# Image 3's routing rounds hold tiles 0, 1 and 2 to 4 in place of 0 to 2 and 3, 4, in a fused embed, attention and expert kernel whose five work orders are laid out anew

## The reference

```python
h = jnp.einsum('bhid,oi,od->bho', x, weighted_sum, weight)
h = jnp.concatenate([h, txt], axis=1)
# attention, on layernorm(h)
gk = jax.nn.log_sigmoid(x @ Wg1 @ Wg2 + bg2).reshape(Bb, Ll, H, D) / GLN
def step(S, inp):
    S = jnp.exp(gk_t)[..., None] * S + k_t[..., None] * v_t[..., None, :]
    o_t = jnp.einsum('bhdv,bhd->bhv', S, q_t) * SCALE
o = o * jax.lax.rsqrt(jnp.mean(o * o, axis=-1, keepdims=True) + EPS) * g_norm_w
o = o.reshape(Bb, Ll, Hid)
h = h + (o * (g * jax.nn.sigmoid(g))) @ Wo
# experts, on layernorm(h)
top_v, top_i = jax.lax.top_k(xf @ Wr, K)                 # K = 2
expv = jnp.exp(top_v - m)
top_p = expv / (jnp.sum(expv, axis=-1, keepdims=True) + 1e-12)
oh = experts[:, None] == jnp.arange(E)[None, :]
pos = jnp.sum(jnp.cumsum(oh.astype(jnp.int32), axis=0) * oh, axis=-1) - 1
kept = pos < cap
xe = jnp.zeros((E, cap + 1, D)).at[experts, pos_safe].set(xf[tokens])[:, :cap]
h2 = jax.nn.silu(xe @ W1) * (xe @ W3)                     # per expert
ye = h2 @ W2
out = jnp.zeros((T, D)).at[tokens].add(wk[:, None] * yp)  # h + out is returned
```

## Time and profile before

| | us |
|---|---|
| median of 3 runs | 599.27 |
| lowest, highest | 598.28, 599.59 |
| the profiled execution, its own time | 594.9 |
| its span, first to last instruction | 593.1 |
| of that: up to the end of attention and routing | 266 |
| `early_up` and the wait behind it | 266 to 282 |
| the eight experts | 282 to 593 |

### The profile page before, as it was taken

One profiled execution on the slowest core, in us unless ns is written; L12 is line 12 of the kernel. 1 busy time (PEld: TensorE's weight loads), 2 busy tenths in 40 slices (PEclk: granted clock), 3 DMA queues, 4 the chain that ended last, 5 costly groups with the idle time before them and its releaser, 6 DMA issues.

```text
span 593.1 us, 13905 instructions
## 1 busy us (share of the span) xinstructions
PE 568.7 (96%) x4846; PEld 531.2 (90%) x4846; DVE 385.0 (65%) x1007; ACT 335.0 (56%) x891; POOL 337.0 (57%) x394
## 2 busy tenths in 40 slices
...
GB/s 266 236 277 123 149 11 51 72 54 23 81 73 64 70 23 65 70 89 110 164 161 90 187 119 7 263 33 71 214 17 186 116 5 264 34 66 77 19 2 48
DMA packets 44587, 60.09 MB, mean 101 GB/s; under 512 B 4529, under 2 KB 33137, under 8 KB 44530
## 3 DMA queue, kind: packets, MB, share of 16 engines
...
...
## 4 chain that ended last, share of the span: by engine, by line
PE 82%; DVE 8%; ACT 3%; issue 3%; DMA 2%; SPq 0%; POOL 0%; DVEq 0%; POOLq 0%; ACTq 0%
PE ps L1950 45%; PE ps L1997 15%; PE ps L2191 3%; PE ps L2177 3%; PE ps L1992 3%; PE ps L2136 2%; PE ps L2172 2%; PE ps L1971 1%; PE ps L2184 1%; DMA sb_x_in<-in_x 1%; PE ps L2152 1%; PE ps L2206 1%; DVE sb_bn L1555 1%; DMA sb_h<-in_txt 1%; PE ps L2225 1%
## 5 line engine op out<-in xcount | busy, mean ns | idle before, releaser
L1950 PE MATMUL ps<-sb_xe_hi,sb_rounded 128*128 128x256 f32 (+1 forms) x1024 | 206.2, 296 | 0.0
L1950 PEld LDWEIGHTS ps<-sb_xe_hi,sb_rounded 128*128 128x128 f32 x1024 | 166.0, 190 | 0.0
L1950 PE MATMUL ps<-sb_xe_lo,sb_rounded 128*128 128x320 f32 (+1 forms) x512 | 151.6, 296 | 0.0
L1950 PEld LDWEIGHTS ps<-sb_xe_lo,sb_rounded 128*128 128x128 f32 x512 | 97.2, 190 | 0.0
L1997 PE MATMUL ps<-sb_rounded,sb_h_hi 128*128 128x256 f32 x512 | 94.2, 285 | 0.0
L1460 DVE TENSOR_TENSOR sb_dec<-ps,sb_gate 128x256 f32<-128x256 f32 (+1 forms) x121 | 55.2, 456 | 54.3 <-ACT sb_gate L1164 51.0
L1164 ACT ACTIVATE sb_gate<-ps 128x256 f32<-128x256 f32 (+1 forms) x121 | 49.2, 406 | 66.3 <-PE ps L1950 65.4
L1997 PEld LDWEIGHTS ps<-sb_rounded,sb_h_hi 128*128 128x128 f32 x512 | 78.4, 189 | 0.0
L998 POOL DMA_INDIRECT out_rows<-sb_att,sb_s_token x40 | 61.8, 1545 | 29.0 <-DVE sb_att L1471 22.6
L1490 DVE TENSOR_TENSOR sb_h_lo<-sb_dec,sb_h_hi 128x256 fp32r<-128x256 f32 x128 | 69.8, 546 | 3.7 <-ACT sb_h_hi L1425 3.2
L1997 PE MATMUL ps<-sb_rounded,sb_h_lo 128*128 128x256 f32 x256 | 72.0, 281 | 0.0
...
## 6 DMA issues: line engine op xcount, KB each, us to landing
...
```

Source lines behind the costliest of these rows:

```text
L1950: ins = pe.matmul(out_ap, lhs, rhs, start=(first and i == 0), stop=(last and i == n - 1))
```

## The change

`ROUNDS` moves tile 2 of image 3 (number 17) from round 4 to round 5, and all five tables of orders are new. The work is the same: the same steps, except that the two rounds have other lengths. Several steps are done by another engine: `ln2_apply` of six tiles goes to ACT from POOL or DVE; of the splits and gated outputs at the start and through the images some go from DVE or ACT to POOL and others back.

```diff
-ROUNDS = [(0, 5), (5, 10), (10, 13), (13, 15), (15, 18), (18, 20)]
+ROUNDS = [(0, 5), (5, 10), (10, 13), (13, 15), (15, 17), (17, 20)]
...
-xn2_turn.3.2@7 attn_out.3.3@6 rank.3@4 router.3.2@5 attn_out.3.4@7 rank.4@6 xn2_turn.3.3@5 xn2_turn.3.4@4 router.3.3@7
-router.3.4@5 early_turn.1@4 early_turn.0@6 early_turn.2@7 rank.5@5 early_up.1@2 early_up.0@0 counts@4 early_up.3@6
...
+xn2_turn.3.2@1 attn_out.3.4@4 router.3.2@6 attn_out.3.3@5 rank.4@7 xn2_turn.3.3@4 xn2_turn.3.4@6 router.3.3@5
+router.3.4@4 rank.5@6 counts@7 early_turn.0@5 early_turn.1@4 early_turn.2@2 early_up.0@0 early_up.1@6 early_up.2@2
...
-x_split.0.2.0 x_split.0.2.1 wo_scale x_split.0.3.0 x_split.1.0.1 x_split.1.1.0 x_split.1.3.1 q_mask.0.0 x_split.2.0.1
...
+we_split.2 we_split.3 x_split.0.2.1 x_split.0.2.0 x_split.0.3.1 x_split.0.3.0 wo_scale x_split.1.0.0 x_split.1.1.1
```

More of the change, by code:

```diff
@@ L55 @@
[L55 to L69, removed]
```

229 lines of the change are left out of this document (122 added, 107 removed).

## The result

The changed kernel takes 600.61 us (median of 19 runs, 596.34 to 603.99) against 597.62 us (19 runs, 593.28 to 600.47) for the kernel before: ratio 1.0056, 95% interval 1.0033 to 1.0079. That is +3.3 us, slower. The forecast was slower by 1.8 us, 601.1 in a range of 596.4 to 604.2; sign and range held, the size was about half of what came. That 601.1 lies so near to 600.61 is luck: the forecast started from 599.27, the median of three runs of the kernel before, and over 19 runs that median is 597.62.

The account below looks back on a forecast made before the run. PE's own work was taken as the bound, except at attention's end, where a chain over DVE, PE and ACT sets the time. Terms 0.5 + 0 + 1.0 - 0.6 + 0.85 = +1.75 gave 601.1 us, range 596.4 to 604.2.

Parts of the forecast that it names:

- (f): End of attention: early_turn goes behind rank.5, slots.5 and counts, so early_up waits on DVE; +3.3 us.
- (a): End of attention: ACT copies turned tiles sooner, PE's last steps close up behind a short wait before mix.3.3; -0.65 us.
- (b): End of attention: limits.4 no longer needs the last tile and its top2 holds two, ending earlier; -1.2 us.
- (d): Round 5 gets three tiles: rank.5 +0.85 us and its top2 +0.4 us.
- (e): End of attention: limits.5 no longer stands behind weigh.5 on DVE; -1.0 us.
- images 0 to 2: Dense stretch up to 157 us: steps swap places and engines, PE's work is unchanged; 0 us.
- Entry of image 3: Text load issued later and scores moved behind it, so PE's next product comes later, with a 1.7 us wait; +1.0 us.
- Turn from image 2 to 3: Wait before head_norm.2.4 goes (-0.9), k_proj.3.1.0 is followed at once by its user (+0.3); -0.6 us.
- The start: POOL does more splits ahead of embed.0.3, delaying it, partly hidden by a later wait; +0.5 us.
- Rival F: Faster: low clock at 147 does not return, start and entry are covered; -1.75 us, median 597.5, chance 0.34.
- Rival S: Slower: new waits at entry and before mix.3.3 lower the clock; 602.8 with one, 604 both partly; chance 0.24 including D.
- D: Before the first expert: the last scatter's end becomes the bound, +2.3 us and more; chance counted inside Rival S.

Follow-up runs that it names:

- turn_early: Changed kernel with early_turn put back ahead of rank.5 and counts behind early_up.1; ratio 0.9999 to the kernel before.
- limits_first: Kernel before with only limits.5 moved ahead of weigh.5 on DVE; ratio 0.9991.
- turn_late: Kernel before with rank.5 and counts ahead of early_turn on PE, and early_turn behind slots.5 and counts on DVE; ratio 1.0057.
- tail_new: Kernel before's orders up to router.3.0, then the changed kernel's orders and rounds; ratio 1.0025 to the kernel before.
- front_new: Changed kernel's orders up to router.3.0, then the orders and rounds of the kernel before; ratio 1.0031 to the kernel before.
- top2_later: turn_early with top2.0 moved on DVE from ahead of mix.1.3 to behind attn_out.1.2; ratio 1.0020 to the kernel before.
- start_old: turn_early with the start's splits and ACT's first eight steps back as in the kernel before; ratio 0.9983 to that kernel.
- state_sooner: top2_later with k_turn.3.2, scores.3.4 and state.3.2 directly behind attn_out.3.1 on PE, ACT and DVE matched; ratio 1.0099 to the kernel before.
- rounds_only: Kernel before with only the ROUNDS line changed, all five orders kept; ratio 1.0004.
- tail_tuned_again: Second measurement: kernel before with limits.5 ahead of weigh.5, slots.3 ahead of router.3.2, top2.4 ahead of attn_out.3.4 on DVE; ratio 0.9989.

## Why the prediction was right, and where it was not

The sign came from step (f), and the tail bears it out. The forecast gave slower a chance of 0.49 only, and about half of the loss comes from terms of the front that it had priced at nothing or as a gain; without them the total would have been near the forecast. The terms of the tail, each read from the traces:

| term | forecast | measured | from |
|---|---|---|---|
| (a) to the end of `router.3.0` | -0.65 | +2.4 | 9.68 to 12.10 |
| (b) wait before `rank.4` | -1.2 | -1.5 | 3.87 to 2.40 |
| (c) `rank.4` of two tiles | -0.85 | -0.84 | 3.40 to 2.56, next step's start |
| (d) `rank.5` of three tiles | +0.85 | +0.85 | 2.55 to 3.40 in `turn_early` |
| (e) `limits.5` ahead | -1.0 | -0.98 | `limits_first` |
| (f) `early_turn` behind `counts` | +3.3 | +3.3, +3.4 | `turn_early`, `turn_late` |
| (d) `top2.5` of three tiles | +0.4 | +0.4 | 260.14 to 261.80, now 262.14 to 264.17 |
| (b) to (f) in all | +1.5 | +1.1 to +1.5, +1.8 | `tail_new`; 22.49 to 24.29 |
| front with (a) | +0.25 | +1.9 to +2.9 | `front_new` |

The steps of (a) lie ahead of `router.3.0`, so the experiments' cut puts them into the front. So counted, the tail was right, and the whole miss is in the front. There the sum was mis-sized, and some of its steps were wrong. Two terms failed: (a), and images 0 to 2.

*(a), priced at -0.65.* The "new short wait before `mix.3.3`" was 2.02 us, and 0.7 us after it the clock fell, so that nearly all of both `mix` steps ran at 1.2 GHz. The stretch from `attn_out.3.2` to the end of `router.3.0` took 11.1 to 12.1 us in the five profiled executions that have this wait (the changed kernel, `front_new`, `turn_early`, `top2_later`, `start_old`), and the clock fell 0.7 to 1.8 us after `mix.3.3` began. In the eight with before's front it took 8.8 to 9.9 us, and the clock fell only after `mix.3.4`. Up to `attn_out.3.2` the five are 0.9 us later in the mean than the eight; with this stretch it is 3.4. That the wait is what brings the fall forward is not shown: `state_sooner` has no such wait, and there the clock fell 4 us ahead of `mix.3.3`, behind waits of 0.85 and 0.72.

*Images 0 to 2, priced at 0.* The waits of 0.67, 1.67 and 0.90 between 100 and 160 and of 1.28 at 47.6 are none that I had found, though my bound from below held only a single wait of 0.87. Reading an order by hand for a dense stretch shows what is next on each engine, not how late DVE is by then. DVE in the changed kernel ran `scores.1.3` (2.28 us), `state`, and the five-tile `top2.0` (4.7 us) ahead of `mix.1.3`, for which PE waited:

```profile
135.45 1.57 DVE L1798 TENSOR_TENSOR sb_raw<-sb_raw,sb_before 128x320 f32<-128x320 f32 x1
137.06 1.46 DVE L1800 TENSOR_TENSOR sb_beaten<-sb_beaten,sb_raw 128x320 f32<-128x320 f32 x1
...
139.19 0.42 DVE L1759 TENSOR_TENSOR sb_og<-ps,sb_gate 128x256 f32<-128x256 f32 x1
```

*Entry of image 3, priced at +1.0: wrong.* PE has no wait there in the changed kernel (5.00 of 5.00 us busy). This was one of the signs by which I said that I would be wrong. I had taken the text load's 5.27 us for its own length. In the changed kernel it is issued 3 us later, at 164.42, and the statistics of the text begin at 166.34:

```profile
166.34 0.42 DVE L1555 BATCH_NORM_STATS2 sb_bn<-sb_h 32x6 f32<-32x256 f32 x1 [0.30 <-DMA sb_h<-in_txt]
```

```profile
157.92 0.91 SPq L805 DMA_DIRECT2D sb_x_in<-in_L_ffn_W  x2
...
164.42 0.33 SPq L884 DMA_DIRECT2D sb_h<-in_txt  x1
```

Before, it was issued 1.5 us behind two weight transfers of 512 KB:

```profile
159.88 1.19 SPq L805 DMA_DIRECT2D sb_x_in<-in_L_ffn_W  x2
161.40 0.33 SPq L884 DMA_DIRECT2D sb_h<-in_txt  x1
```

Now it is 6.5 us behind them, and takes 1.9 us. That it had to stand behind them in the queue is my reading of this. With before's order unchanged there, the wait itself differs from one execution to the next, with the time of the load: 4.5 us and no wait in `limits_first`, 4.8 and 0.34 in `tail_new`, 5.3 and 0.87 before, 5.7 and 1.85 in `turn_late`, 5.8 and 1.91 in `rounds_only`. So the wait that I moved about varies by 1.9 us by itself.

*Turn from image 2 to 3.* The wait of 0.88 went, as forecast; in its place stand 0.26, 0.49 and 0.37 us, where I had +0.3. From image 3's range sum to `attn_out.3.2` it takes 0.56 us less, and -0.6 was forecast. *The start:* in the profiled execution `embed.0.3` came 1.2 us later and the wait behind it fell by 1.0.

*Rival F.* Its clock part came in this execution (neither 24 nor 147 fell), and the mean clock of `front_new` over its 12 runs fits it. In this execution it was worth nothing in the sum, because the stretch at the end lasted 37.5 us in place of 30.7: after a wait of 1.51 us `early_up` ran 5.3 us at the lower clock, before 3.8. *Rival S.* Its second half, the fall drawn forward over the `mix` steps, is what the five executions show, at 1.8 us of a price of up to 4. Its first half, a stretch behind a long wait at the entry, has two examples, both with before's order there: in `turn_late` the wait of 1.85 at 169.12 was followed by 6.8 us at 1.2 GHz from about 171.8 on, and in `tail_tuned_again` one of 1.75 at 171.48 by 10.2 us. But `rounds_only` had 1.91 us there, and nothing followed until 213, so the length of a wait alone does not decide it. *D.* The last scatter ended at 278.0, not near 273.5 as I had it: it began 2.3 us later than before, behind `slots.5`, and has two DMAs more. The first expert still came 9.9 us behind it, and its wait is 1.39 us on DVE in both kernels, so D cost nothing.

What stays open: why DVE is late at 135 to 140 and 156 to 160 in the changed front. `top2_later` moved one step there and gained nothing, `state_sooner` moved others further on and lost, and no run separates the three engines' moves. Open too is why the lower clock begins where it does.
